# Self-attention and transformer as one program for each engine, and the start of the self-attention in the drain of the cross attention

## The reference, cut to what matters

```
x = x + cross_attention(ctx, latents=x, mask)       # 16 heads of 64, keys from 4096 tokens and the latents, layer norm inside
z = layernorm(x);  Q, K, V = z @ Qw, z @ Kw, z @ Vw # self-attention, one head of 256
x = x + softmax(causal(Q @ K^T / 16)) @ V
y = layernorm(x)
for layer in 2 layers:                              # transformer: 8 heads of 64, windows of 128
    q, k, v = heads(shift_token(y) @ wqkv); l2-normalise, rotate q and k
    y = y + local_attention(q, k, v) @ wo
    h = layernorm(shift_token(y)) @ w1 + b1;  y = y + (a * gelu(g)) @ w2 + b2
out = y + x
```

## Time and profile before

| | us |
|---|---|
| time, median of 3 runs | 1114.54 (1112.46 to 1114.59) |
| the profiled execution's own time / its span | 1115.23 / 1113.4 |
| cross stage, to the last addition to x | 0 to 680.8 |
| self-attention, to the last addition to x | 681.1 to 732.5 |
| transformer, to the first TENSOR_REDUCE f_sums_raw | 733.0 to 748.6 |
| the rest of the transformer | 748.6 to 1113.4 |

### The profile page before, as it was taken

One profiled execution on the slowest core, in us unless ns is written; L12 is line 12 of the kernel. 1 busy time (PEld: TensorE's weight loads), 2 busy tenths in 40 slices (PEclk: granted clock), 3 DMA queues, 4 the chain that ended last, 5 costly groups with the idle time before them and its releaser, 6 DMA issues. The chain is left out here.

```text
span 1113.4 us, 25515 instructions
## 1 busy us (share of the span) xinstructions
PE 1030.5 (93%) x8616; PEld 953.4 (86%) x8617; DVE 830.4 (75%) x3048; ACT 655.1 (59%) x1516; POOL 216.3 (19%) x259
## 2 busy tenths in 40 slices
PE   3899999999999999999999985867999999999977
PEld 3789999999999989999999985746788898989976
DVE  5897777796777796777787765558988889888642
ACT  4566565674566674656665562426676776767732
POOL 0111111111111110111111113900006203263222
PEclk9999999999999999999999996978999999999997
DMA  5000000000000000000000003400001000110001
GB/s 194 22 3 11 11 1 0 12 11 3 11 1 1 12 11 3 11 1 10 3 11 4 2 1 104 118 1 1 1 17 43 1 2 20 33 45 2 2 1 39
DMA packets 29455, 21.70 MB, mean 19 GB/s; under 512 B 13652, under 2 KB 26920, under 8 KB 29352
## 3 DMA queue, kind: packets, MB, share of 16 engines
q1 hardware_dynamic: 28368, 20.22, 6.1%
q10 hardware_dynamic: 984, 0.13, 0.1%
HBM read 19.23 MB, written 1.05 MB: 18 GB/s over the span
## 5 line engine op out<-in xcount | busy, mean ns | idle before, releaser
L260 PEld LDWEIGHTS pv_ps<-v,pt 128*128 128x128 f32 x1792 | 214.3, 191 | 8.4 <-issue 3.6
L260 PE MATMUL pv_ps<-v,pt 128*128 128x65 f32 x1792 | 214.8, 271 | 2.0 <-DVE o L693 1.9
L671 DVE CUSTOM_DVE_ANT_0 s_sb<-s_ps,pen,mstate 128x256 f32<-128x256 f32 (+1 forms) x512 | 199.9, 447 | 13.6 <-issue 10.7
L437 ACT ACTIVATE probs<-s_sb,mbias 128x256 f32<-128x256 f32 (+1 forms) x512 | 203.2, 470 | 0.1
L565 POOL TENSOR_TENSOR o<-o,alpha 128x260 f32<-128x260 f32 x128 | 85.5, 668 | 573.1 <-ACT alpha L431 573.1
L446 ACT ACTIVATE pt<-turn 128x512 f32<-128x512 f32 x128 | 76.3, 596 | 120.7 <-PE turn L247 108.5
L247 PE MATMUL turn<-ident,probs 128*128 128x128 f32 x896 | 123.5, 278 | 4.2 <-DVE ql L649 2.1
L247 PEld LDWEIGHTS turn<-ident,probs 128*128 128x128 f32 x896 | 98.3, 144 | 14.3 <-issue 2.6
L693 DVE TENSOR_TENSOR o<-o,pv_ps 128x260 f32<-128x260 f32 x128 | 54.0, 422 | 49.9 <-PE pv_ps L260 39.1
L236 PE MATMUL s_ps<-kh,qh 64*128 64x256 f32 (+1 forms) x512 | 79.1, 305 | 4.2 <-DVE kl L643 1.8
L643 DVE TENSOR_TENSOR kl<-proj,kh 128x512 fp32r<-128x512 f32 (+1 forms) x63 | 41.2, 655 | 51.4 <-ACT kh L424 51.1
(11 more groups left out here) (301 smaller groups left out, 2796.3 us busy)
## 6 DMA issues: line engine op xcount, KB each, us to landing
raw<-in_ctx SPq DMA_DIRECT2D x24, 128.0 KB, 2.1
f_wqkv_raw<-in_L_ffn_wqkv SPq DMA_DIRECT2D x6, 512.0 KB, 4.2
wkv_raw<-in_L_xattn_Wkv SPq DMA_DIRECT2D x2, 1024.0 KB, 8.1
f_w_raw<-in_L_ffn_w SPq DMA_DIRECT2D x8, 256.0 KB, 5.8
f_w_raw<-in_L_ffn_w SPq DMA_DIRECT2D x2, 640.0 KB
wq_raw<-in_L_xattn_Wq SPq DMA_DIRECT2D x1, 1024.0 KB, 8.1
wout_raw<-in_L_xattn_Wout SPq DMA_DIRECT2D x1, 1024.0 KB, 10.2
f_wo_raw<-in_L_ffn_wo SPq DMA_DIRECT2D x2, 512.0 KB, 5.2
```

The source lines that it names most:

```text
L260: last = pe.matmul(t.pv_ps[:, u, :], t.pt[g % 2][:, u, kt, :], t.v[:, kt, h, :], start=(kt == 0), stop=(kt == kts - 1))
L437: last = act.activation(t.probs[g % 2][:, u, 0:kts * P], t.s_sb[g % 2][:, u, 0:kts * P], ACT.Exp, bias=t.mbias[:, at:at + 1], scale=0.125)
L671: last = dve.tensor_tensor_reduce(out=t.s_sb[g % 2][:, u, 0:width], in0=t.s_ps[g % 2][:, u, 0:width], in1=t.pen[:, 0:width], scale=1.0, sc ...
```

## The change

The programs of the self-attention and the transformer become one, `latent_stage`, with no end of block between them; and part of the self-attention goes into the last two steps of the cross stage. `attend_stage` is taken out.

In the last `half` step DVE makes the moments of batches 0 to 2 (6 tiles; their `x` is final by then) and normalises them, PE transposes batches 0 and 1; in the drain PE transposes batch 2 and projects Q, K and V of batch 0 (36 matmuls of 256 columns), ACT and DVE split the transposes, the three weights (loaded by SP behind the last tokens) and Q and K of batch 0. These use banks and buffers of the cross stage: `t.turn`, `t.proj`, the places of wq, qh, ql and raw. SP loads 3 more tiles there.

In the new program the self-attention goes batch by batch, batches 1 to 3 projected while the scores and softmax of the ones before run; every product is now of one batch, so Q and K are 256 columns wide. Batch 3 is normalised and transposed there. The layer norm for `y` is made for batch 0 in the middle and for batches 1 to 3 (6 tiles) at the end; the first unit's transposes and split stand in front of the last batch's addition. The constants are set by POOL, in front of its splitting of the weights; only the padding is zeroed, not the whole tiles; the weights' loads no longer wait for that, but for w2. The loop over T is the same, from T = 0 on PE. `y` lies in the place of raw, one set of head buffers in that of wq.

The cross stage's part, and the new functions:

```diff
+def turn_mid(pe, t, s, b, bank):
+
...
+    for kc in range(KC):
+        for q in range(QT):
+            last = pe.transpose(bank[:, kc * L + q * P:kc * L + (q + 1) * P], t.raw[:, 1 + b, q, kc * P:(kc + 1) * P], t.ident[:])
+    last.then_inc(s["mid_turned"], 1)
...
+def project_mid(pe, t, s, b, w, bank):
+
+    for m in range(KC):
+        for kc in range(KC):
+            last = split_product(pe, bank[:, m * L:(m + 1) * L], [part[:, KC * w + kc, m * P:(m + 1) * P] for part in t.late],
+                                 [x[:, kc, b * L:(b + 1) * L] for x in t.mid_xt], kc == 0, kc == KC - 1)
+    last.then_inc(s["mid_qk_done"], 1)
...
+def values_mid(pe, t, s, b, bank):
+
+    for q in range(QT):
+        for kc in range(KC):
+            last = split_product(pe, bank[:, q * D:(q + 1) * D], [x[:, kc, b * L + q * P:b * L + (q + 1) * P] for x in t.mid_xt],
+                                 [part[:, 2 * KC + kc, :] for part in t.late], kc == 0, kc == KC - 1)
+    last.then_inc(s["mid_v_done"], 1)
...
+            for k, name in enumerate("QKV"):
+                sp.dma_start(t.late_raw[:, KC * k:KC * k + KC, :], args[f"L0_attn_{name}w"].rearrange("(k p) n -> p k n", p=P)
+                             ).then_inc(s["next_w_loaded"], 16)
...
+                    if final and j in (5, 7):
+                        if j == 5:
+                            pe.wait_ge(s["pt_ready"], 16 * m)
+                            turn_mid(pe, t, s, 0, t.turn[1])
+                        else:
+                            pe.wait_ge(s["k_ready"], 4 * m + 4)
+                            turn_mid(pe, t, s, 1, t.proj)
+                    if kind is None and j == 1:
+                        pe.wait_ge(s["mid_xt"], 1)
+                        turn_mid(pe, t, s, 2, t.turn[1])
+                    if kind is None and j == 3:
+                        pe.wait_ge(s["next_w"], 2)
+                        pe.wait_ge(s["s_done"], 8 * m)
+                        pe.wait_ge(s["mid_xt"], 2)
+                        project_mid(pe, t, s, 0, 0, t.proj)
+                        pe.wait_ge(s["mid_xt"], 3)
+                        project_mid(pe, t, s, 0, 1, t.turn[1])
+                    if kind is None and j == 6:
+                        pe.wait_ge(s["next_w"], 3)
+                        pe.wait_ge(s["pt_ready"], 16 * m)
+                        values_mid(pe, t, s, 0, t.turn[0])
...
+                    if final and j == 2:
+                        next_deviations()
+                    if final and j == 6:
+                        next_xt_hi(0, t.turn[1])
+                        next_weights_hi(0)
+                    if kind is None and j == 0:
+                        next_xt_hi(1, t.proj)
+                        next_weights_hi(1)
+                    if kind is None and j == 2:
+                        next_xt_hi(2, t.turn[1])
+                        next_weights_hi(2)
+                    if kind is None and j == 5:
+                        next_qk_hi(m, 0, t.proj)
+                        next_qk_hi(m, 1, t.turn[1])
+                        next_store_values(t.turn[0])
...
+            def next_moments():
+                dve.wait_ge(s["x_added"], 2 * B)
+                for k in range(TILES - QT):
+                    last = dve.bn_stats(t.x_stats[:, k, :], t.x[:, k, :])
+                last.then_inc(s["next_step"], 1)
...
+                for k in range(TILES - QT):
+                    last = dve.bn_aggr(t.x_mv[:, k, :], t.x_stats[:, k, :])
+                last.then_inc(s["next_step"], 1)
...
+            def next_normed(b):
+                dve.wait_ge(s["next_step"], 4)
+                for k in range(QT * b, QT * b + QT):
+                    last = dve.tensor_scalar(t.raw[:, 1 + b, k % QT, :], t.x[:, k, :], t.x_mv[:, k, 0:1], t.x_rstd[:, k:k + 1],
+                                             ALU.subtract, ALU.mult)
+                last.then_inc(s["next_z"], 1)
...
+                    if kind is None and j == 1:
+                        next_xt_lo(1, t.proj)
+                        next_weights_lo(1)
+                    if kind is None and j == 2:
+                        next_xt_lo(2, t.turn[1])
+                    if kind is None and j == 3:
+                        next_weights_lo(2)
...
                     if final:
+                        if j == 0:
+                            next_moments()
+                        elif j in (3, 5, 6):
+                            next_normed({3: 0, 5: 1, 6: 2}[j])
+                        if j == 7:
+                            next_xt_lo(0, t.turn[1])
+                            next_weights_lo(0)
```

```diff
+            for piece in weight_pieces(t, args, 0):
+                if piece[0] == "w2":
+                    sp.wait_ge(s["pads_zero"], 1)
+                load_piece(sp, s, piece)
+            load_parameters(sp, nc, t, s, args)
...
+            pool.memset(t.zero[:], 0.0)
+            pool.memset(t.log8[:], math.log(8.0))
+            pool.memset(t.ones[:], 1.0)
+            pool.memset(t.mv_up[:], 0.0)
+            pool.memset(t.stats[:], 0.0)
+            pool.memset(t.b1[:], 0.0)
+            for part in t.w2:
+                pool.memset(part[:, HB - 1, :].bitcast(F32), 0.0)
+            for part in t.w1:
+                for side in range(2):
+                    last = pool.memset(part[:, :, side * 768 + HID:side * 768 + 768].bitcast(F32), 0.0)
+            last.then_inc(s["pads_zero"], 1)
+            pool.wait_ge(s["pads_zero"], 1)
+            for k in (6, 9):
+                pool.memset(t.stats[0:1, :, 0, k:k + 1], 64.0)
+            pool.memset(t.wide[:], 0.0)
+            for part in t.xt:
+                pool.memset(part[:].bitcast(F32), 0.0)
+            pool.memset(t.v[:, :, :, LDH:LDH + 1], 1.0).then_inc(s["constants_set"], 1)
+            for piece in weight_pieces(t, args, 0):
+                split_piece(pool, s, piece, 0)
+            pool.wait_ge(s["params_loaded"], 16 * PARAM_LOADS)
...
+                if at == 0:
+                    pe.wait_ge(s["mid_x"], B)
                 if at:
...
+            def mid_scores(b):
+                pe.wait_ge(s["mid_qk"], 2 * b + 2)
+                if b >= 2:
+                    pe.wait_ge(s["mid_s_read"], b - 1)
...
+            mid_project(1, 0)
+            mid_project(1, 1)
+            mid_scores(0)
+            turn_mid(pe, t, s, 3, t.turn[1])
+            mid_values(1)
+            mid_project(2, 0)
+            mid_turn_probs(0)
+            mid_project(2, 1)
+            mid_scores(1)
+            mid_weighted(0)
+            mid_values(2)
+            mid_project(3, 0)
+            mid_turn_probs(1)
+            mid_project(3, 1)
+            mid_scores(2)
+            mid_weighted(1)
+            mid_values(3)
+            mid_scores(3)
+            mid_turn_probs(2)
+            mid_weighted(2)
+            mid_turn_probs(3)
+            turn_latents(0, t.g[0])
+            mid_weighted(3)
+            for T in range(0, UNITS + 3):
...
+            mid_deviation()
+            mid_qk_hi(1, 0)
+            mid_qk_hi(1, 1)
+            mid_xt_hi(3)
+            mid_exponentials(0)
+            mid_store_values(1)
+            mid_qk_hi(2, 0)
+            mid_qk_hi(2, 1)
+            mid_exponentials(1)
+            mid_store_values(2)
+            act.wait_ge(s["constants_set"], 1)
+            first_deviations(1, slice(0, QT))
+            mid_qk_hi(3, 0)
+            mid_qk_hi(3, 1)
+            mid_exponentials(2)
+            mid_store_values(3)
+            mid_exponentials(3)
+            latents_hi(0, t.g[0])
+            first_deviations(2, slice(QT, TILES))
             for T in range(-1, UNITS + 3):
                 if valid(T - 1):
                     exponentials(T - 1, 1, 1)
...
+            mid_moments()
+            mid_normed()
+            mid_qk_lo(1, 0)
+            mid_qk_lo(1, 1)
+            mid_maxima(0)
+            mid_xt_lo(3)
+            mid_qk_lo(2, 0)
+            mid_store_turned(0)
+            mid_qk_lo(2, 1)
+            mid_maxima(1)
+            mid_add(0)
+            first_moments(1, range(0, QT))
+            mid_qk_lo(3, 0)
+            mid_store_turned(1)
+            first_normed(1, range(0, QT))
+            mid_qk_lo(3, 1)
+            mid_maxima(2)
+            mid_add(1)
+            mid_maxima(3)
+            mid_store_turned(2)
+            mid_add(2)
+            mid_store_turned(3)
+            latents_lo(0, t.g[0])
+            mid_add(3)
+            first_moments(2, range(QT, TILES))
+            first_normed(2, range(QT, TILES))
+            dve.wait_ge(s["constants_set"], 1)
+            dve.wait_ge(s["params_loaded"], 16 * PARAM_LOADS)
             for T in range(-1, UNITS + 3):
```

411 lines of the change are left out of this document (199 added, 212 removed).

## The result

The changed kernel takes 1085.43 us (median of 4, 1083.92 to 1086.10) against 1114.57: ratio 0.9735, 95% interval 0.9711 to 0.9759, some 29 us less. The forecast was 1089, range 1080 to 1098. The profiled execution took 1083.92, its span is 1082.0; it was the fastest of the four, so the two profiles lie 31.4 apart in span where the medians lie 29.1 apart. In 3 of its 52 executions the kernel before took 1105 to 1106 us instead of 1112 to 1119, and one of it at 1451.8, like one of e4 at 1965.3, is left out of all figures here.

A forecast was written before the change was run, and what follows sets the result against it. The seams before and after the self-attention were taken as latency, not throughput. Span 1113.4 − 28.4 (seam) + 3.0 (drain) = 1088.0; from the median, 1114.54 − 25.4 = 1089.1, so forecast 1089 us, range 1080 to 1098.

The forecast's parts named there:

- drain: End of the cross stage, up to its last addition to x: added preparation costs +3.0 us, range 0 to +7.
- seam: From the cross stage's last addition to x to the transformer loop's first TENSOR_REDUCE: 67.8 us becomes 39.4, a gain of 28.4.
- rest: Remaining 364.8 us of the span, from the first TENSOR_REDUCE on: order of instructions left alone, no change forecast.
- B1: PE from the cross stage's end to batch 3's scores: 156 matmuls, transposes, products and waits, 24.0 us.
- B2: Tail of batch 3 in the self-attention, with nothing left to fill it: 10.1 us, including 2.4 for the port.
- B3: From x to the first rotation: moments, logarithm and exponential, ACT's copies and squares, 5.3 us.
- The rival of a half clock: Waits between batches keep PE at half clock for most of the projection stream: 1098 to 1102 us, chance 0.10.
- The port's price: DVE's waits for POOL in the self-attention: two biases on the path at half of 2.38 each, 2.4 us.
- The rival built on it: Self-attention: each DVE instruction between SBUF and SBUF waits for a whole POOL one; slower than before, 1118 us, chance 0.03.
- POOL as the bound: Rival: POOL's 37 us grows by 4 to 6, tables delay the first rotation; 1091 to 1093 us, chance 0.10.
- A: Kernel before, from the cross stage's last addition to the loop's first TENSOR_REDUCE: 67.8 us.
- B: The same distance in the new kernel, summed from three parts: 39.4 us, bounds 35.5 to about 50.

The follow-up runs named there:

- e4: Changed kernel with DVE's normalisation of the last six tiles and ACT's logarithm and exponential for them moved later in the first unit; 1083.11 us.
- e5: Changed kernel run once more, unchanged, as a control; 1086.08 us.
- e3: Changed kernel with POOL zeroing the low parts of the first layer's weights instead of computing them; 1084.62 us.
- e1: Changed kernel with all its preparation for the self-attention put behind the cross stage's last addition to x; 1097.94 us.
- e2: Kernel before, with 16 and 12 unread matmuls in front of two of PE's waits in the drain; 1105.64 us, ratio 0.995.
- e8: Kernel before, with unread matmuls or transposes filling PE's waits in drain, self-attention and first unit; 1106.80 us, ratio 0.9939.

## Why the prediction was right, step by step

- **The size.** −25.4 was forecast, −29 came. By the profiles: seam −30.8 (forecast −28.4), drain +1.9 (forecast +3.0), rest −2.4 (forecast nothing). The main mechanism, a seam in which PE streams and the preparation is hidden in the drain, came as forecast; that the seam's sum came so near is in part luck, since the parts' misses, B1 1.1 and B2 2.2 too long and B3 1.0 too short, partly cancel. Of the signs named, two were missed narrowly: the last addition of the self-attention came 30.8 behind the seam and not 32 to 36, and the tables were ready 0.3 behind the start of the first TENSOR_REDUCE and not before it.
- **B1, PE's stream**, 24.0: the last of its matmuls ends at 705.43, 22.9 behind the seam. The sum of 156 matmuls at full clock held, and of the 1.5 allowed for waits 0.3 came (682.53 to 682.85). The rival of a half clock did not come in the stream, since PE was fed throughout (10.00 of 10 from 690); in the tail it came in the profile of e5, and cost the wait for one batch's products 1.4.
- **B2, the tail**, 10.1: 7.9 (705.43 to 713.28). The 2.4 that I put on the biases were too much: those of batches 2 and 3 took 0.56 and 0.66.
- **B3, to the rotation**, 5.3: 6.3. I followed the path over ACT's copies and squares, and that path took 5.4 (713.28 to 718.64), as forecast. What I did not add are the six normalisations, which stand in front of the reduction in DVE's order. Without the port they end just as early, 5.4 behind the addition (e3, 712.12 to 717.49), so leaving them out cost nothing by itself; beside POOL's low parts they took 1.0 longer, and that is the 6.3. In e5 they took 2.31, and the distance was 5.6. e4's −2.4 in the seam does not separate the two paths, since it shortens both. The port's price, 2.4 in the forecast, was 1.5 by e3 (0.8 here, 0.7 ahead of the last addition), and mostly on other instructions than the biases.
- **The Trainium skill** ("SBUF — State Buffer", "Who interferes with whom") has the port as an exclusive lock. The trace agrees: 3.11 for 0.73, 2.41 for 1.22, 4.53 for 1.38, each beside POOL's low parts. The rival built on it, that every such instruction waits for a whole one of POOL and the kernel gets slower, did not come: most of what DVE does here reads PSUM and kept its length (0.55 for a copy of 128x384).
- **POOL as the bound**: did not come, by 0.9 us. The tables were ready 37.3 behind the seam's start, where 37 was forecast. e4 shows that it stands right behind: 1.47 of wait as soon as DVE is earlier.
- **The drain**, +3.0: +1.9 against the kernel before, +3.0 against e1, where the same program runs without the preparation in the drain. The slip behind the moments was 1.5 (640.44 against 639.14, forecast 1.6), and gone at 643.01 (643.15 before). Against a drain without preparation and with full clock (e2) it is 5.2.
- **What the sum lacked** is the clock in the seam. I cut A as a whole from the trace, half clock and all, and B at full clock; the gain came out, but its reason was incomplete: about 6 of 30.8 are clock (e8). Of the 2.4 in the rest, 1.0 falls between the first and the third TENSOR_REDUCE (20.57 before, 19.54 after), where the kernel before has 0.69 in 760 to 770, and 0.9 between the sixth and the seventh (23.24 and 22.34), around its 0.83 in 810 to 820. By their place these are clock too, but no run isolates them, and in e5 the rest is only 1.1 below the kernel before's.

## What to carry to other kernels

At a seam between stages, follow the chain from the last write of the one to the first steady instruction of the other in each engine's own order, not in one alone: two paths here were equally long, and the one that I left out was the one that a wait for the port could lengthen. Count the clock of both sides of such a seam, since a wait costs twice, once itself and once in the matmuls behind it, and where the half clock falls can move by microseconds with a change elsewhere, and even between two executions of one kernel. Profile the same kernel twice before you read anything into a microsecond. When an engine or a port is nearly the bound, moving its work in time moves the wait (tables, product, normalisation: 1.5, 1.7, 3.2 us) and does not remove it.
